# Three-part transformer kernel: first normalisations moved to GpSimd beside the attention, other gates before the last scatters, token rows in eights, an earlier bias matmul

## The reference, cut to what matters

```python
# x: (8, 128, 32, 32) -> tokens (8, 1024, 128)
qkv = (tokens @ w_proj + b_proj); attn = softmax(q k^T / 4) over keys, 8 heads of 16
t = attn_out @ w_out + b_out + tokens                    # part 1: attention
z = _ln_t(t)                                             # layer norm, eps 1e-5
s_q, s_k, s_v = (z @ Wq.T >= 0.25), (z @ Wk.T >= 0.25), (z @ Wv.T >= 0.3)
mask = causal & (s_q s_k^T > 0.1); t = t + mask @ s_v    # part 2: spikes
z2 = _ln_t(t); prob = softmax(z2 @ Wr + br); e = argmax(prob)
y = gelu(z2 @ W1[e] + b1[e]) @ W2[e] + b2[e]             # part 3: one of 8 experts a token
t = t + y * (p_max / p_max)                              # part 4: result, turned back to (8, 128, 1024)
```

## Time and profile before

| what | value |
|---|---|
| median of 3 runs | 1201.19 us (1200.94 to 1204.97) |
| the profiled execution | 1193.27 us, its span 1191.5 us |
| attention | 0 to 835.3 us of the span |
| middle part | 835.6 to 1014.9 us |
| expert part | 1014.9 to 1163.0 us |
| result part | 1163.0 to 1191.5 us |
| PE busy over the span | 1090.2 us (92%) |
| DVE, ACT, POOL busy | 880.9, 783.0, 302.3 us |

### The profile page before, as it was taken

One profiled execution on the slowest core, in us unless ns is written; L12 is line 12 of the kernel. 1 busy time (PEld: TensorE's weight loads), 2 busy tenths in 40 slices (PEclk: granted clock), 3 DMA queues, 4 the chain that ended last, 5 costly groups with the idle time before them and its releaser, 6 DMA issues. The chain is left out here.

```text
span 1191.5 us, 23759 instructions
## 1 busy us (share of the span) xinstructions
PE 1090.2 (92%) x8048; PEld 533.4 (45%) x8048; DVE 880.9 (74%) x2012; ACT 783.0 (66%) x1698; POOL 302.3 (25%) x364
## 2 busy tenths in 40 slices
PE   5999999999999999999999999999789972899994
PEld 2223333333333333333333333334565652899983
DVE  4899889978988987987988898851567654455545
ACT  2167777777777877787777787786576431455553
POOL 4131041031013104104102210010325556344450
PEclk7599999999999999999999999999898875899996
DMA  5529008206504702800830550000600111222219
GB/s 132 111 54 163 22 16 175 47 8 139 98 2 96 141 1 54 162 22 2 174 62 2 109 110 2 2 19 1 175 8 30 32 35 58 59 68 71 71 55 284
DMA packets 73356, 85.53 MB, mean 72 GB/s; under 512 B 15656, under 2 KB 57256, under 8 KB 71704
## 3 DMA queue, kind: packets, MB, share of 16 engines
q1 hardware_dynamic: 64248, 72.65, 28.1%
q0 software_dynamic: 4320, 8.89, 2.3%
q10 hardware_dynamic: 4672, 2.49, 0.9%
HBM read 57.08 MB, written 26.65 MB: 70 GB/s over the span
## 5 line engine op out<-in xcount | busy, mean ns | idle before, releaser
L730 DVE TENSOR_REDUCE neg_half<-slot 128x1 f32<-128x512 f32 x1024 | 633.9, 682 | 101.8 <-PE slot L505 84.2
L644 ACT ACTIVATE probs<-ring 128x512 f32<-128x512 f32 x1024 | 528.7, 603 | 135.7 <-PE ring L514 133.4
L514 PE MATMUL ring<-stack_q,stack_k 50*128 50x512 bf16 (+1 forms) x2048 | 420.2, 383 | 1.9
L556 PE MATMUL acc<-probs,v_sb 128*32 128x512 f32 x2048 | 272.7, 605 | 0.0
L514 PEld LDWEIGHTS ring<-stack_q,stack_k 50*128 50x128 bf16 (+1 forms) x2048 | 152.2, 93 | 257.3 <-issue 109.6
L507 PE MATMUL slot<-twin_k,twin_q 48*128 48x512 bf16 x512 | 183.0, 392 | 20.4 <-DMA twin_q<-parts_dram 12.4
L505 PE MATMUL slot<-stack_k,stack_q 48*128 48x512 bf16 x512 | 162.5, 393 | 2.8 <-DVE neg_half L730 2.8
L1571 ACT ACTIVATE zt<-bank,b_of 128x128 f32<-128x128 f32 x284 | 80.9, 368 | 80.3 <-PE bank L1539 80.3
L424 POOL CAST m_parts<-neg_max 128x16 bf16<-128x16 f32 x32 | 6.3, 197 | 380.4 <-DVE neg_max L736 380.4
L507 PEld LDWEIGHTS slot<-twin_k,twin_q 48*128 48x128 bf16 x512 | 47.6, 93 | 95.1 <-DVE neg_half L730 72.8
L1514 POOL DMA_INDIRECT rows_tok<-zt,x_in x71 | 68.2, 960 | 80.1 <-DVE zt L1599 77.8
(11 more groups left out here) (161 smaller groups left out, 1099.5 us busy)
## 6 DMA issues: line engine op xcount, KB each, us to landing
parts_dram<-parts SPq DMA_DIRECT2D x30, 384.0 KB, 5.7
stack_k<-parts_dram SPq DMA_DIRECT2D x16, 384.0 KB, 6.0
stack_q<-parts_dram SPq DMA_DIRECT2D x32, 192.0 KB, 7.3
x_in<-rows_in SPq DMA_DIRECT2D x71, 64.5 KB
xp<-in_x SPq DMA_DIRECT2D x8, 512.0 KB, 4.8
stack_k<-parts_dram SPq DMA_DIRECT2D x16, 256.0 KB, 3.6
xr<-in_x SPq DMA_DIRECT2D x8, 512.0 KB, 4.6
out<-zt SPq DMA_DIRECT2D x16, 256.0 KB, 2.1
```

The costliest lines, as they stand in the source:

```text
L514: return pe.matmul(out[:, :], stack_k[s % STACK_BUFS][rows, h, kt * P:(kt + 1) * P], stack_q[s % STACK_BUFS][rows, half, h, :], start=star ...
L556: mm = pe.matmul(acc[32 * h:32 * h + 32, :], v_sb[s // G % 2][:, kt, s % G * HG + h, :], probs[:, j % PROBS, h, :], start=(kt == 0), stop= ...
L644: act.activation(probs[:, j % PROBS, h, :], ring[n % S_BANKS][:, :], ACT.Exp).then_inc(s_empty[n % S_BANKS], 1)
L730: dve.tensor_reduce(neg_half[q % 2][:, half, k:k + 1], slot[n % M_BANKS][:, :], AX.X, ALU.max, negate=True).then_inc(m_empty[n % M_BANKS], 1)
```

## The change

1. In the attention, behind its last `max_parts`, POOL waits until the first seven batches have their means and variances and until the last `v` projection has read `xp`. Then `normalise` runs: a memset of `power`, eps added to 56 variances, one `pow` on 128x56, and 16 tiles (batches 0 and 1) normalised into `z`. The two buffers of `z` are now those of `xp`, which the attention loads its input into.
2. The head of the middle part loses DVE's and ACT's work on the root, DVE's 8 tiles of batch 0, and POOL's and ACT's 8 of batch 1. The root of batch 7 alone is taken by POOL with `pow` on 128x8. PE's order: the turns of batch 0 first, then the three weights. ACT's order: two copies of `zt`, `w_t`, then its four tiles of batch 2.
3. `scatter(5, 7)` no longer waits for `s_shift2`. `scatter(6, 2)` and its successor wait for ACT's copy of the last `turn2` where they waited for the logits and the difference; `s_less` and `s_sum` are no longer gates.
4. The bias matmul of the logits is issued ahead of the wait for ACT's copies of `turn2`.
5. Token numbers go by eights: partition p of a batch holds tokens 8p to 8p + 7, where it held four of each half. The 16 loads of the result part become 9: two halves of batch 0, then seven whole batches; SP issues five, ACT four.

```diff
@@ attention_kernel, end of gpsimd
+            pool.wait_ge(s_aggr, OUTS * (B - 1))
+            wait_filled(pool, ("v", (B - 1, 1)))
+            normalise(pool)
@@ middle_stage, gpsimd
-        pool.wait_ge(s_rstd1, 1)
-        z_of(1)
+        pool.wait_ge(s_var1, 1)
+        pool.tensor_tensor(rstd1[:, LAST], var1[:, LAST], power[:, LAST], ALU.pow).then_inc(s_rstd1, 1)
+        z_of(2)
...
-        z_of(2)
...
-        count_up(z_all[:, :, C].bitcast(I32).rearrange("p (n q) -> p n q", q=4), [[HALF, 2 * B], [1, 4]], 0, 4)
+        count_up(z_all[:, :, C].bitcast(I32).rearrange("p (n q) -> p n q", q=KT), [[N, B], [1, KT]], 0, KT)
...
         scatter(B - 3, 6)
-        pool.wait_ge(s_shift2, B)
         scatter(B - 3, 7)
         wait_filled(pool, ("turn2", B - 1, 0))
         scatter(B - 2, 0)
         wait_filled(pool, ("turn2", B - 1, 1))
         scatter(B - 2, 1)
+        wait_taken(pool, ("turn2", B - 1, 1))
+        scatter(B - 2, 2)
+        scatter(B - 2, 3)
         pool.wait_ge(s_logit, B)
-        scatter(B - 2, 2)
-        pool.wait_ge(s_less, B)
-        scatter(B - 2, 3)
+        scatter(B - 2, 4)
         pool.wait_ge(s_exp, B)
-        scatter(B - 2, 4)
+        scatter(B - 2, 5)
         pool.wait_ge(s_chosen, B)
-        scatter(B - 2, 5)
-        pool.wait_ge(s_sum, B)
         scatter(B - 2, 6)
         scatter(B - 2, 7)
@@ middle_stage, tensor: logits(b)
-            for j in range(2):
-                wait_taken(pe, ("turn2", b, j))
             if b:
                 pe.wait_ge(s_less, b)
             out = ps_logit
             pe.matmul(out[:, :], one_row[:, :], b_r[:, :, :].rearrange("o k e -> o (k e)"), start=True, stop=False)
+            for j in range(2):
+                wait_taken(pe, ("turn2", b, j))
@@ middle_stage, tensor and scalar: order at the head
+                if job == ("turn", 0, 1):
+                    weights()
...
-                if job == ("turn", 1, 1):
+                if job == ("turn", 0, 1):
+                    weights()
+                    act.wait_ge(s_shift1, 1)
                     for k in range(POOL_Z, KT):
                         z_of(2, k)
@@ middle_stage, vector: head
-        dve.tensor_scalar(std1[:, :], mv[:, :, 1], LN_EPS, None, ALU.add).then_inc(s_var1, 1)
-        dve.wait_ge(s_std1, 1)
-        dve.reciprocal(rstd1[:, :], std1[:, :]).then_inc(s_rstd1, 1)
+        dve.tensor_scalar(var1[:, LAST], mv[:, LAST, 1], LN_EPS, None, ALU.add).then_inc(s_var1, 1)
+        others = slice(0, (B - 1) * KT)
+        dve.scalar_tensor_tensor(out=shift1[:, others], in0=mv[:, others, 0], scalar=-1.0, in1=rstd1[:, others],
+                                 op0=ALU.mult, op1=ALU.mult).then_inc(s_shift1, 1)
         dve.wait_ge(s_rstd1, 1)
-        for k in range(KT):
-            dve.tensor_scalar(z[0][:, k, :], t_all[:, k, :], mv[:, k:k + 1, 0], rstd1[:, k:k + 1],
-                              ALU.subtract, ALU.mult).then_inc(s_z0, 1)
...
+        dve.scalar_tensor_tensor(out=shift1[:, LAST], in0=mv[:, LAST, 0], scalar=-1.0, in1=rstd1[:, LAST],
+                                 op0=ALU.mult, op1=ALU.mult).then_inc(s_shift1, 1)
@@ result_stage
+    LOADS = [(0, KT // 2), (KT // 2, KT // 2)] + [(b * KT, KT) for b in range(1, B)]
...
-        eng.dma_start(z_all[:, 4 * n:4 * n + 4, 0:C],
-                      rows_tok[4 * n * P:(4 * n + 4) * P, :].rearrange("(p q) c -> p q c", q=4)).then_inc(s_back[n], 16)
+        t, count = LOADS[n]
+        b, q = t // KT, t % KT
+        eng.dma_start(z_all[:, t:t + count, 0:C],
+                      rows_tok[b * N:(b + 1) * N, :].rearrange("(p q) c -> p q c", q=KT)
+                      [:, q:q + count, :]).then_inc(s_back[n], 16)
@@ build
+        def normalise(pool):
+
+            cols = slice(0, (B - 1) * KT)
+            pool.memset(power[:, :], -0.5).then_inc(s_first, 1)
+            pool.tensor_scalar(var1[:, cols], mv_a[:, cols, 1], LN_EPS, None, ALU.add).then_inc(s_first, 1)
+            pool.wait_ge(s_first, 2)
+            pool.tensor_tensor(rstd1[:, cols], var1[:, cols], power[:, cols], ALU.pow).then_inc(s_first, 1)
+            pool.wait_ge(s_first, 3)
+            for t in range(2 * KT):
+                pool.tensor_scalar(z[t // KT][:, t % KT, :], t_all[:, t, :], mv_a[:, t:t + 1, 0], rstd1[:, t:t + 1],
+                                   ALU.subtract, ALU.mult).then_inc(s_first, 1)
```

More of the change, by code:

```diff
@@ L198, in attention_kernel @@
 def attention_kernel(nc, sb, psum, sem, x, w_proj, b_proj, w_out, b_out, t_all, mv, ident, identb, parts_dram,
-                     load_more):
-    xp = [sb(f"xp{i}", [P, N], F32) for i in range(2)]
+                     load_more, normalise, xp):
     xr = sb("xr", [P, N], F32)
@@ L877, in scalar_z, with middle_stage @@
 def scalar_z(b):
[L879 to L882 removed]
+    return (KT - POOL_Z) * (b == 2) + (KT * (b - 1) - POOL_Z) * (b > 2)
+def middle_stage(nc, sb, psum, sem, w_raw, s_raw, wr, br, t_all, z_all, mv, var1, rstd1, power, z,
+                 ident, rows_in, tails, p_max, gain, slot_expert,
                   slot_start, slot_row, tail_row, s_sent, s_tail, s_table, load_weights):
@@ L893, in middle_stage @@
     var2 = sb("var2", [P, TILES], F32)
-    power = sb("power", [P, KT], F32)
     rstd2 = sb("rstd2", [P, TILES], F32)
     shift2 = sb("shift2", [P, TILES], F32)
-    z = [sb(f"z{i}", [P, KT, C], F32) for i in range(2)]
     zt = [sb(f"zt{i}", [P, N], F32) for i in range(2)]
@@ L1079, in tensor, with weights @@
     def tensor(pe):
-        pe.wait_ge(s_raw, 48)
-        for n in range(3):
-            mm = pe.transpose(bank[RING - 1][:, n * C:(n + 1) * C], w_raw[:, n, :], ident[:, :])
-        mm.then_inc(s_wt, 1)
-        pe.wait_ge(s_wc, 1)
+        def weights():
+            pe.wait_ge(s_raw, 48)
+            for n in range(3):
+                mm = pe.transpose(bank[RING - 1][:, n * C:(n + 1) * C], w_raw[:, n, :], ident[:, :])
+            mm.then_inc(s_wt, 1)
+            pe.wait_ge(s_wc, 1)
         def free_bank(job):
@@ L1093, in turn @@
             _, b, j = job
-            if b == 0:
-                pe.wait_ge(s_z0, 4 * j + 4)
-            elif j == 0 and b <= 2:
-                pe.wait_ge(s_zp, b * POOL_Z)
-            else:
+            if b == 2 and j == 0:
+                pe.wait_ge(s_zp, POOL_Z)
+            elif b >= 2:
                 pe.wait_ge(s_za, scalar_z(b) - 4 * (1 - j))
@@ L1237, in exp, with weights @@
             act.activation(prob[:, :, :], logit[:, :, :], ACT.Exp).then_inc(s_exp, 1)
-        act.wait_ge(s_wt, 1)
-        act.activation(w_t[:, :, :], bank[RING - 1][:, 0:3 * C].rearrange("p (n c) -> p n c", n=3),
-                       ACT.Copy).then_inc(s_wc, 1)
-        act.wait_ge(s_var1, 1)
-        act.activation(std1[:, :], std1[:, :], ACT.Sqrt).then_inc(s_std1, 1)
-        act.wait_ge(s_shift1, 1)
-        for k in range(POOL_Z, KT):
-            z_of(1, k)
+        def weights():
+            act.wait_ge(s_wt, 1)
+            act.activation(w_t[:, :, :], bank[RING - 1][:, 0:3 * C].rearrange("p (n c) -> p n c", n=3),
+                           ACT.Copy).then_inc(s_wc, 1)
         for job in STAGE:
@@ L1453, in vector @@
         table()
-        step(dve.reciprocal(std1[:, :], p_max[:, :]))
-        dve.tensor_tensor(gain[:, :], p_max[:, :], std1[:, :], ALU.mult)
+        step(dve.reciprocal(shift1[:, :], p_max[:, :]))
+        dve.tensor_tensor(gain[:, :], p_max[:, :], shift1[:, :], ALU.mult)
     def all_taken(eng):
@@ L1623, in result_stage @@
     ps = bank[0:RINGS]
-    s_back = [sem(f"o_back{i}") for i in range(2 * B)]
+    LOADS = [(0, KT // 2), (KT // 2, KT // 2)] + [(b * KT, KT) for b in range(1, B)]
+    s_back = [sem(f"o_back{i}") for i in range(len(LOADS))]
     s_add = sem("o_add")
@@ L1643, in vector @@
     def vector(dve):
-        for t in range(TILES):
-            dve.wait_ge(s_back[t // 4], 16)
-            dve.scalar_tensor_tensor(out=t_all[:, t, :], in0=z_all[:, t, 0:C], scalar=gain[:, t:t + 1],
-                                     in1=t_all[:, t, :], op0=ALU.mult, op1=ALU.add).then_inc(s_add, 1)
+        for n, (first, count) in enumerate(LOADS):
+            dve.wait_ge(s_back[n], 16)
+            for t in range(first, first + count):
+                dve.scalar_tensor_tensor(out=t_all[:, t, :], in0=z_all[:, t, 0:C], scalar=gain[:, t:t + 1],
+                                         in1=t_all[:, t, :], op0=ALU.mult, op1=ALU.add).then_inc(s_add, 1)
     def tensor(pe):
@@ L1660, in scalar @@
         all_told(act)
-        for n in range(1, 2 * B, 2):
+        for n in range(1, len(LOADS), 2):
             load(act, n)
@@ L1670, in sync @@
         all_told(sp)
-        for n in range(0, 2 * B, 2):
+        for n in range(0, len(LOADS), 2):
             load(sp, n)
@@ L1699, in build @@
         w_raw = sb("w_raw", [P, 3, C], F32)
+        var1 = sb("var1", [P, TILES], F32)
+        rstd1 = sb("rstd1", [P, TILES], F32)
+        power = sb("power", [P, TILES], F32)
```

(3 more changed lines are left out.)

25 lines of the change are left out of this document (9 added, 16 removed).

## The result

The kernel after took 1196.16 us (median of 14 executions, 1192.81 to 1201.58) against 1203.61 (14, 1200.30 to 1206.29) for the kernel before, run beside it: ratio 0.994, 95% interval 0.9925 to 0.9956. It is faster by 7.4 us; the interval allows 5.3 to 9.0. The profiled execution of after took 1197.78 us.

A forecast was written before the change was run, and what follows sets the result against it. PE bounds the attention, a line of single steps the middle part, DMA the result part. Head 3.5, round 0 0.9, tail 3.1 and result 0 sum to 7.5 us off 1201.19: 1193.7 us, range 1189.5 to 1198.5.

The forecast's parts named there:

- Head: Start of the middle part: first spike matmul at 839.3 against 842.8, a gain of 3.5 us.
- the upper end, 4.7: Head of the middle part: gain of 4.7 us if PE's earlier start brings the clock rise before the spikes.
- Round 0: First round of the middle part: ACT's four batch 2 tiles leave the chain, gaining 0.9 us, ends 0 and 1.5.
- My replay of PE's list: Round 0: with ACT 1.5 us earlier, PE becomes the bound and reaches its second pair some 0.9 earlier.
- Tail: End of the middle part: POOL's scatters run without a stop, gaining 3.1 us, ends 2.4 and 3.9.
- the count of slots: Tail: scatters from scatter(5, 6) on, 1.26 us each, put scatter(7, 0) at 1000.0 against 1003.12.
- GpSimd's new work: Attention: added POOL work hidden before the barrier, cost 0, with 18.1 us of cover left over.
- eights: Result part: new token order and coarser loads, taken as 0 us, with -1.4 as the end.
- Faster loads: Result part: fewer, larger loads reach 381 GB/s, 14.3 us becoming 11.0; gain 10.8, time 1190.4; chance 0.08.
- Late GpSimd: Barrier at 835: GpSimd arrives late, slower than before; at 1.0 us a column time 1220; chance 0.04.
- Terms paid in part: Head and result part: clock rises no earlier, DVE's 1.4 us reaches the end; gain 4.4, time 1196.8; chance 0.22.
- A stage behind takes it back: Rounds paced by something that does not shift, or other waits replace the gain; gain 2, time 1199; chance 0.06.

The follow-up runs named there:

- e3: Kernel before with only token numbers by eights and nine loads in the result part; ratio 0.9997, 1203.76 us.
- e5: Kernel before again, with no edit, for a second profile; ratio 1.0001, 1199.24 us.
- e7: Kernel before with SP reading its eight tail rows in one load instead of eight; ratio 0.9994, 1199.17 us.
- e2: Kernel before with only the new gates of the last scatters and the bias ahead of the wait; ratio 0.9997, 1204.53 us.
- e6: Kernel after with SP reading its eight tail rows in one load instead of eight; ratio 0.9931, 1191.28 us, on another chip.
- e8: Kernel after with ACT's four tiles of batch 2 back behind batch 1's copies; ratio 0.9979, 1196.92 us, on another chip.
- e12: Kernel after a third time, unchanged, as comparison for the runs beside it; ratio 0.9937, 1195.82 us.
- e1: Kernel after without its tail and result edits: old scatter gates, old bias place, fours, old result part; ratio 0.9941, 1197.59 us.
- e4: Kernel after again, with no edit, for a second profile and time; ratio 0.9951, 1197.48 us.
- e9: Kernel after with the tail rows read in one load and stored by ACT's queue instead of SP's; ratio 0.9886, 1190.53 us.
- e10: Kernel after with SP's eight tail rows waiting until every scatter has landed; ratio 0.9962, 1201.03 us.
- e11: Kernel before with the three weight transposes at the head done eight times over (24 for 3); ratio 1.0047, 1208.82 us.

## Why the prediction was right, and where it was not

The time was right to 2.5 us and the gain, 7.4 us for 7.5, to 0.1. The terms were not: two were too small and one was not paid. That their errors cancel to 0.1 is luck; the head and round 0, forecast at 4.4, have the whole gain.

**Head, forecast 3.5, measured 4.6 to 4.9.** The mis-sized part is the sentence that the eight transposes run at the low clock: they took 1.06 us, not 2.24, and the weights 0.49, not 0.89. That is 1.6 of PE work, of which 1.5 shows: the first spike follows PE's first step by 2.19 us, not 3.7. I had taken the clock of that place from one execution. It was at 0.50 there in the first profile of before and in e3, and at 0.97 to 1.00 in e5 (whose three weight transposes took 0.53), e7, e2 and all eight profiles with the new head. Behind it, the clock of the first spikes differs between executions of the same kernel: in after, e6, e8 and e12 it fell to 0.50 for some 3 us, in e1, e4, e9 and e10 it stayed at 1.00. A window of e1:

```profile
840.00:842.00 2.00, 1.21 (x7) 0.73 (x6) 0.12 (x1) 2.00 (x6) 2.00 (x3) 1.00 0.29 35
```

and one of e5, a kernel with the old head:

```profile
842.00:844.00 2.00, 1.91 (x6) 1.22 (x6) 0.16 (x1) 1.79 (x4) 2.00 (x11) 0.50 1.01 362
```

The high clock is worth 1.5 us more (first mask at 9.45 for 10.9 to 11.05, pos 0 at 44.5 for 46.0). All five profiles with the old head and its usual weights began the spikes at 0.50. The first spike thus came as early as the upper end, 4.7, had it, but by another way: I had put the 1.2 above the middle down to a high clock in the spikes, and it came from the transposes ahead of them.

**Round 0, forecast 0.9, measured 1.5** (e8). My replay of PE's list let PE become the bound too early; ACT's four tiles were on the path in full. Head and round 0 together: pos 0 stood at 51.1 to 52.7 in the five traces with the old head, and at 44.5 to 46.1 in the seven with the new one and early tiles, 51.7 against 45.2 in the mean, 6.6 us where I had 4.4. The head alone timed 7.1 us (e1).

**Tail, forecast 3.1, measured 0.** POOL did what the count of slots says. What failed is the sentence that SP is ready 0.8 before the scatters: it rested on the trace's 1011.4 in an execution in which no step of SP was slow. In all nine other profiles with SP's unchanged tail code beside scatters, the eight stores take 14.2 to 16.7 us (8.13 in that one). With the new gates `pos` to `x_in` even grows: 20.5 to 20.8 us in the five traces with the new gates and SP's unchanged tail code, against 15.1 to 17.9 in the five with the old ones. Why the steps are slower there is not shown: behind `pos` the scatters start every 1.26 us, all but one, with the old gates and with the new. The bias gives 0.57 of that back in the last round (13.06 for 13.63). By time, e2 shows neither my 3.1 of gain nor the 3 of loss that the traces add up to: 0.9997, that is -2.3 to +1.4 us. The timed executions have no trace, so whether profiling itself makes SP's steps slower stays open. That SP's path hides the earlier scatters is borne out by e9: with the registers loaded at once and the stores taken off SP, a further 5.3 us come.

**GpSimd's new work, forecast 0, and eights, forecast 0:** both held. Measured were 22 us left over at the barrier, and 0.9997 for e3. The rule on the shared ports of the Trainium skill ("SBUF — State Buffer", "Who interferes with whom") was not tried by this: in after, DVE stood idle for 19.37 us up to 813.29, and POOL's tiles ended at 816.15. The two DVE instructions that fall beside the last tiles took 0.26 and 0.42 us, as the same two did at 793.21 and 793.50, ahead of POOL's new work. The barrier stands at 835.3 to 837.8 with the old head and at 835.7 to 841.6 with the new, 1.1 later in the mean. That spread goes with the time for which PE's clock was at 0.50 before the barrier: 44.4 us in e5, e7, e6, e10 and e12 (barrier 835.7 to 836.2, the three with the new head the earlier ones), 51.2 in e11, e2, e1, after and e4 (837.6 to 840.5), 58.0 in e9 (841.6). A cost of POOL's work beside the attention does not show in it, but within the second group e4 is 1.7 to 2.9 us later than the others, so a cost of 1 us could not be told.

**Rivals.** Faster loads: no, 297 GB/s for 294. The Trainium skill's rule in "DMA: Bandwidth & Descriptors", "Bandwidth", that larger DMAs move faster, did not show here for loads of 512 KB in pieces of about 500 bytes. Late GpSimd: no. "Terms paid in part" named the wrong terms: its low clock did not cost the head its gain, and DVE's wait was not 1.4. "A stage behind takes it back" is what happened to the tail, by SP's queue, a wait that I had priced at 0.8 and not looked at further.

## What to carry to other kernels

One profile is one execution. A term that rests on another engine being ready a little earlier (0.8 us here) needs that engine's steps in a second profile, or its own range. Small register steps and DMA issues that run beside a dense row of indirect DMAs can take 0.7 us each: load the registers at once, put them on an idle queue, or let the engine that needs the result next do something else meanwhile. The same holds for the clock under PE's first work behind a barrier: it is a range, not the level of one profile.

## What the runs showed of the hardware

- SP's and ACT's register steps (0.02 to 0.5 us in the first profile of before) came in multiples of 0.70 us while scatters were in flight (after, 998.8 to 1011.2), and at their usual length from 3.3 to 3.5 us behind the last scatter's issue (six traces) or when they began only then (e10). Scatters in flight are needed but do not suffice: the first profile of before had none of it, and ACT in e9 sent its first rows quickly beside scatters. What sets it off is open.
- `pow` on GpSimd: 1.67 us for 128x8, 9.32 for 128x56; an estimate from these two is 0.16 us a column over a fixed 0.4.
- PE's clock at the same place of the same kernel differed between executions (0.50 or 1.00 at the first spikes: after and e12 against e4), worth 1.5 us.
- The attention's length went with the time for which PE's clock was low: the barrier at 835.7 to 836.2 with 44.4 us at 0.50, at 837.6 to 840.5 with 51.2, at 841.6 with 58.0.
